# The broadcast of C in a state-space scan: full precision matmuls from one copy of its rows, and C first in every step

## The reference, cut to what matters

```
x (4,256,256), ctx (4,256,128);  DI = 256 channels, DS = 16 states, L = 256 times
u      = silu(causal_conv4(in_proj @ ctx))                  per batch: 256 channels x 256 times
B, C   = x_proj @ u                                         16 rows each, x 256 times
delta  = softplus(dt_proj @ (x_proj_dt @ u) + bias)
state[t] = state[t-1] * exp(delta[t] * A) + delta[t] * u[t] * B[t]     for every channel and state n
y[t]   = sum over n of state[t] * C[t]  + D * u[t]
x1     = x + y * silu(layernorm(x))
logits = layernorm(x1) @ Wg;  the best 2 of 8 experts by softmax, at most 320 rows for each
out    = x1 + sum over the 2 of weight * (relu(row @ w1) @ w2)
```

## Time and profile before

| | |
|---|---|
| median of 3 runs | 289.02 us (288.33 to 290.1) |
| the profiled execution, its own time | 288.53 us |
| its span, first to last instruction | 286.7 us |
| busy: PE, DVE, ACT, POOL | 84%, 75%, 61%, 74% of the span |
| mean granted clock of TensorE | 0.93 of full speed |

### The profile page before, as it was taken

One profiled execution on the slowest core, in us unless ns is written; L12 is line 12 of the kernel. 1 busy time (PEld: TensorE's weight loads), 2 busy tenths in 40 slices (PEclk: granted clock), 3 DMA queues, 4 the chain that ended last, 5 costly groups with the idle time before them and its releaser, 6 DMA issues.

```text
span 286.7 us, 5022 instructions
## 1 busy us (share of the span) xinstructions
PE 239.6 (84%) x1564; PEld 218.4 (76%) x1564; DVE 216.1 (75%) x372; ACT 174.1 (61%) x379; POOL 213.5 (74%) x174
## 2 busy tenths in 40 slices
PE   8967597867957396678699999999999999999970
PEld 7745476545845285557589999999999999999960
DVE  3799999999799999999978757566675738383620
ACT  2899759777886776669326357463747465564400
POOL 1689899669976999998744668687777777777561
PEclk9999959995999957589999999999999999999995
DMA  6679520080002805043032675745544454544110
GB/s 158 236 224 330 215 120 0 5 305 25 0 1 67 303 0 187 0 145 112 21 129 74 205 235 186 231 169 205 174 178 169 178 173 179 213 181 182 38 59 24
DMA packets 15073, 40.38 MB, mean 141 GB/s; under 512 B 2922, under 2 KB 9900, under 8 KB 12112
## 3 DMA queue, kind: packets, MB, share of 16 engines
q1 hardware_dynamic: 11792, 33.15, 33.9%
q0 software_dynamic: 2816, 6.32, 6.6%
q10 hardware_dynamic: 448, 0.70, 0.9%
HBM read 32.72 MB, written 8.49 MB: 144 GB/s over the span
## 4 chain that ended last, share of the span: by engine, by line
PE 39%; issue 4%; DVE 4%; DMA 2%; POOL 2%; ACT 1%; POOLq 1%; SPq 0%; ACTq 0%
PE ps L1064 12%; PE ps L1065 11%; PE ps L1066 11%; DVE h L1291 2%; PE ps L1073 2%; PE ps L1080 2%; DVE hc L1303 1%; DMA xe<-expert_rows 1%; DMA expert_rows<-xrow,sloti 1%; POOL expert_rows L403 1%; POOL so_far L482 1%; POOL out L491 1%; DMA out<-eo,dst 1%; POOLq L108 1%; DVE eo L1497 0%
## 5 line engine op out<-in xcount | busy, mean ns | idle before, releaser
L358 POOL TENSOR_TENSOR dbu<-du,bsb 128x1024 f32<-128x1024 f32 x31 | 72.7, 2366 | 1.2 <-DMA bsb<-b_rows 1.0
L582 ACT ACTIVATE ps<-delta,anegs 128x255 f32<-128x255 f32 x128 | 53.0, 461 | 14.4 <-DVE h L1284 10.7
L1486 DVE SCALAR_TENSOR_TENSOR htlo<-ps,hthi 128x320 fp32r<-128x320 f32 x64 | 30.4, 487 | 37.8 <-ACT hthi L748 37.8
L847 PE MATMUL ps<-stack,sels 64*128 64x256 f32 x64 | 17.2, 355 | 34.9 <-DVE hc L1303 32.1
L847 PEld LDWEIGHTS ps<-stack,sels 64*128 64x128 f32 x64 | 11.0, 215 | 42.7 <-issue 42.3
L472 POOL TENSOR_TENSOR w2lo<-w2raw,w2hi 128x512 fp32r<-128x512 f32 x28 | 35.9, 1302 | 9.0 <-ACT w2hi L643 8.8
L869 PE MATMUL ps<-cst,hc 128*128 128x128 f32 x256 | 40.7, 310 | 1.4 <-DVE hc L1303 1.4
L1284 DVE TENSOR_TENSOR_SCAN h<-ps,dbu 128x1024 f32<-128x1024 f32 x18 | 41.1, 2283 | 0.4 <-POOL dbu L358 0.3
L1064 PE MATMUL ps<-xthi,w1hi 128*128 (+1 forms) x124 | 39.3, 317 | 0.3 <-ACT w1hi L636 0.3
L748 ACT ACTIVATE hthi<-ps 128x320 fp32r<-128x320 f32 x64 | 28.0, 437 | 18.6 <-PE ps L1066 18.6
L1303 DVE TENSOR_TENSOR hc<-h,ps 128x1024 f32<-128x1024 f32 x31 | 37.1, 1197 | 2.6 <-issue 2.0
(11 more groups left out here) (185 smaller groups left out, 510.4 us busy)
## 6 DMA issues: line engine op xcount, KB each, us to landing
w1raw<-in_w SPq DMA_DIRECT2D x8, 1024.0 KB
w2raw<-in_w SPq DMA_DIRECT2D x8, 1024.0 KB, 4.9
bsb<-b_rows SPq DMA_DIRECT2D x7, 1024.0 KB, 6.6
expert_rows<-fill SPq DMA_DIRECT2D x1, 2580.0 KB, 15.8
xe<-expert_rows SPq DMA_DIRECT2D x8, 258.0 KB, 5.1
out<-x SPq DMA_DIRECT2D x4, 256.0 KB, 5.1
xnat<-in_x SPq DMA_DIRECT2D x1, 768.0 KB, 7.3
xe<-expert_rows SPq DMA_DIRECT2D x8, 64.5 KB, 5.2
```

The source lines that it names most:

```text
L358: nc.gpsimd.tensor_tensor(dbu[j % DRING][:], du[:, :, None, cols(b)].to_broadcast([P, EC, 2, L]), bsb[b % 2][:, None, 2 * p:2 * p + 2, :]. ...
L582: ins = nc.scalar.activation(decays(g % SLOTS_DA)[:, c, i * L + 1:(i + 1) * L], delta[:, c, b * L + 1:(b + 1) * L], ACT.Exp, scale=anegs[: ...
L1486: nc.vector.scalar_tensor_tensor(out=htlo[:, f, :], in0=ps[:, f % 4, 0:CAP], scalar=0.0, in1=hthi[:, f, :].bitcast(F32), op0=ALU.max, op1= ...
```

## The change

The rows of B and C are copied once, in full precision, by one ScalarE instruction (`copy_rows`); `hi_rows`, `lo_rows` and the doubled projection go. C is spread by full precision matmuls from 32 rows. On TensorE c_cast(g+1) now stands first in the step, ahead of `logits` and `counts`, and the convolution is cut into three pieces (p = 3, 4, 5). The bank of its own goes to the last step but one, whose mult comes ahead of the last scan. The sum of the exponentials comes from ScalarE's accumulator, and GpSimd takes the inverse (a power of -1) and multiplies (`weigh`). Where other lines of the diff only follow from these, they are left out.

```diff
 def c_bank(g):
-    return WBANK if g == STEPS - 1 else CBANK
+    return WBANK if g == STEPS - 2 else CBANK
...
-        sels = sm("sels", [XPC, BC], F32R)
-        stack = sm("stack", [XPC, T], F32R)
-        brow = sm("brow", [XPC, L])
+        sels = sm("sels", [BC, BC])
+        rows = sm("rows", [BC, T])
...
+            def weigh(b):
+                pool.wait_ge(s["top_exp"], b + 1)
+                pool.wait_ge(s["const_done"], 1)
+                tiles = tiles_of(b)
+                nc.gpsimd.tensor_tensor(rsum[:, tiles], rsum[:, tiles], none1[:, tiles], ALU.pow
+                                        ).then_inc(s["sum_inverse"], 1)
+                pool.wait_ge(s["sum_inverse"], b + 1)
+                nc.gpsimd.tensor_tensor(xrow[:, tiles, :, DM], etop[:, tiles, 0:TOPK],
+                                        rsum[:, tiles, None].to_broadcast([P, BT, TOPK]), ALU.mult
+                                        ).then_inc(s["gates_done"], 1)
...
                 if b == 2 and p in (1, 5):
                     if p == 1:
                         pool.wait_ge(s["xe_filled"], 16)
+                        weigh(0)
                     send(0 if p == 1 else 1)
+                if b == 3 and p == 2:
+                    weigh(1)
                 if b == 3 and p in (2, 3):
                     send(p)
                 drive(j)
...
+            weigh(B - 2)
             for j in tiles_range(B - 2):
                 send(j)
...
-            def hi_rows(b):
-                nc.scalar.activation(stack[:, cols(b)], ps[0:XPC, XBANK[b], 0:L], ACT.Copy).then_inc(s["hi_done"], 1)
-
-            def b_rows(b):
+            def copy_rows(b):
                 act.wait_ge(s["xp_psum"], b + 1)
-                if b:
-                    act.wait_ge(s["brow_out"], 16 * b)
-                nc.scalar.activation(brow[0:DS, :], ps[0:DS, XBANK[b], 0:L], ACT.Copy).then_inc(s["brow_done"], 1)
+                nc.scalar.activation(rows[:, cols(b)], ps[0:BC, XBANK[b], 0:L], ACT.Copy).then_inc(s["rows_done"], 1)
...
                     ins = nc.scalar.activation(etop[:, j, :], top[:, j, :], ACT.Exp, bias=ntop[:, j:j + 1],
-                                               scale=rx[:, j:j + 1])
+                                               scale=rx[:, j:j + 1], accum_out=rsum[:, j:j + 1])
...
             def c_cast(g):
                 b, p = divmod(g, PAIRS)
-                pe.wait_ge(s["stack_done"], b + 1)
-                if g == STEPS - 1:
+                pe.wait_ge(s["rows_done"], b + 1)
+                if g == STEPS - 2:
                     pe.wait_ge(s["zt_done"], B)
+                elif g == STEPS - 1:
+                    pe.wait_ge(s["mult_done"], g - 1)
                 elif g:
                     pe.wait_ge(s["mult_done"], g)
...
-                                           stack[:, cols(b)], start=(i == 0), stop=True, skip_group_check=True)
+                                           rows[:, cols(b)], start=(i == 0), stop=True, skip_group_check=True)
...
             for g in range(STEPS):
                 b, p = divmod(g, PAIRS)
                 nb = b + 1
+                if g + 1 < STEPS - 1:
+                    c_cast(g + 1)
+                if g == STEPS - 3:
+                    c_cast(STEPS - 1)
                 if b >= 1:
                     if p == (3 if b == B - 1 else 4):
                         logits(b - 1)
                     if p == (4 if b == B - 1 else 6):
                         counts(b - 1)
-                if g + 1 < STEPS - 1:
-                    c_cast(g + 1)
-                if g == STEPS - 3:
-                    c_cast(STEPS - 1)
...
-                if b + 2 < B and p in (3, 4):
+                if b + 2 < B and p == 3:
                     pe.wait_ge(s["sp_t"], nb + 1)
-                    conv(b + 2, p - 3, WBANK)
+                    conv(b + 2, 0, WBANK, range(0, 3))
+                if b + 2 < B and p == 4:
+                    conv(b + 2, 0, WBANK, range(3, TAPS))
+                    conv(b + 2, 1, WBANK, range(0, 2))
+                if b + 2 < B and p == 5:
+                    conv(b + 2, 1, WBANK, range(2, TAPS))
...
             scan(0)
-            lo_rows(0)
             for g in range(STEPS):
                 b, p = divmod(g, PAIRS)
-                if g + 1 < STEPS:
+                if g < STEPS - 2:
                     scan(g + 1)
-                mult(g)
+                    mult(g)
+                else:
+                    mult(g)
+                    if g + 1 < STEPS:
+                        scan(g + 1)
                 nb = b + 1
-                if nb < B:
-                    if p == (1 if b else 2):
-                        lo_rows(nb)
...
-                    if p == (5 if b == B - 1 else 7):
-                        sum_weights(b - 1)
```

More of the change, by code:

```diff
@@ L57 @@
 BC = 2 * DS
-XPC = 2 * BC
 WP = 4
@@ L129, in build @@
         nhalf = sb("nhalf", [P, TILES])
+        none1 = sb("none1", [P, TILES])
         stats = sb("stats", [P, TILES, 6])
@@ L174, in build @@
         ctxs = sm("ctxs", [DC, T])
-        xps = sm("xps", [P, EC, XPC])
+        xps = sm("xps", [P, EC, BC])
         u = sm("u", [P, EC, T])
@@ L244, in spread_b @@
             def spread_b(b):
-                sp.wait_ge(s["brow_done"], b + 1)
-                sp.dma_start(b_dram[b], brow[0:DS, :]).then_inc(s["brow_out"], 16)
+                sp.wait_ge(s["rows_done"], b + 1)
+                sp.dma_start(b_dram[b], rows[0:DS, cols(b)]).then_inc(s["brow_out"], 16)
                 sp.wait_ge(s["brow_out"], 16 * (b + 1))
@@ L319, in _ @@
             nc.gpsimd.memset(nhalf[:], -0.5)
+            nc.gpsimd.memset(none1[:], -1.0)
             nc.gpsimd.memset(fill[:, 0:DM + 1], 0.0)
@@ L450, in _ @@
             pool.wait_ge(s["xe_in"], 32)
[L451 to L454, removed]
+            weigh(B - 1)
             pool.wait_ge(s["gates_done"], B)
@@ L785, in x_proj @@
             def x_proj(b, c, bank):
-                return nc.tensor.matmul(ps[0:XPC, bank, 0:L], xps[:, c, :], u[:, c, cols(b)],
+                return nc.tensor.matmul(ps[0:BC, bank, 0:L], xps[:, c, :], u[:, c, cols(b)],
                                         start=(c == 0), stop=(c == EC - 1))
@@ L808, in first_dt, with conv @@
                 return ins
-            def conv(b, c, bank):
+            def conv(b, c, bank, taps=range(TAPS)):
                 acc = by_chunk(bank)[:, c, :]
-                for k in range(TAPS):
+                for k in taps:
                     ins = nc.tensor.matmul(acc[:, k:L], cwb[:, TAPS - 1 - k, c * P:(c + 1) * P],
@@ L815, in conv @@
                                            stop=(k == TAPS - 1), skip_group_check=True)
-                if c == EC - 1:
+                if c == EC - 1 and taps[-1] == TAPS - 1:
                     ins.then_inc(s["conv_psum"], 1)
@@ L846, in c_cast @@
                     n = DS + 2 * p + i
-                    ins = nc.tensor.matmul(ps[:, c_bank(g), i * L:(i + 1) * L], sels[:, n:n + 1].to_broadcast([XPC, P]),
-                                           stack[:, cols(b)], start=(i == 0), stop=True, skip_group_check=True)
+                    ins = nc.tensor.matmul(ps[:, c_bank(g), i * L:(i + 1) * L], sels[:, n:n + 1].to_broadcast([BC, P]),
+                                           rows[:, cols(b)], start=(i == 0), stop=True, skip_group_check=True)
                 ins.then_inc(s["c_psum"], 1)
@@ L961, in _ @@
             conv(1, 0, YBANK)
[L962 to L963 removed]
+            pe.wait_ge(s["sel_in"], 16)
             c_cast(0)
@@ L991, in _ @@
                 add_state(g).then_inc(s["ysum_done"], 1)
-                if b == B - 1 and p in (2, 3, 4, 5):
+                if b == B - 1 and p in (2, 3, 4, 5, 6):
                     if p == 2:
                         pe.wait_ge(s["fill_made"], 1)
-                    add_zeros((4, 4, 6, 2)[p - 2])
+                    add_zeros((4, 4, 6, 2, 6)[p - 2])
                 if b == 0 and p == 1:
@@ L1211, in z_variance @@
                 ins.then_inc(s["z_stats"], 1)
-            def lo_rows(b):
-                dve.wait_ge(s["hi_done"], b + 1)
-                dve.wait_ge(s["brow_done"], b + 1)
-                nc.vector.tensor_tensor(stack[BC:2 * BC, cols(b)], ps[BC:2 * BC, XBANK[b], 0:L],
-                                        stack[BC:2 * BC, cols(b)].bitcast(F32), ALU.subtract
-                                        ).then_inc(s["stack_done"], 1)
             def softplus_t(b, bank):
@@ L1388, in place @@
                 nc.vector.tensor_copy(sloti[:, tiles, :], slot).then_inc(s["slots_done"], 1)
-            def sum_weights(b):
-                tiles = tiles_of(b)
-                dve.wait_ge(s["top_exp"], b + 1)
-                link(nc.vector.tensor_reduce(rsum[:, tiles], etop[:, tiles, :], AX.X, ALU.add))
-                nc.vector.reciprocal(rsum[:, tiles], rsum[:, tiles]).then_inc(s["weights_sum"], 1)
             def low_w1(e, m):
@@ L1453, in _ @@
             place(last)
-            sum_weights(last)
```

33 lines of the change are left out of this document (9 added, 24 removed).

## The result

The changed kernel takes 310.81 us (median of 4 runs; 288.97 for the kernel before beside them), a ratio of 1.0751 with an interval of 1.0707 to 1.0795. Forecast was 295.3, with a range of 291 to 299: the direction was right, but the rise of 6.3 that was forecast is less than a third of the one that came. The profiled span is 308.4, 21.7 more than the 286.7 of before.

What follows compares the result with a forecast made beforehand. VectorE was taken to bound the scan stage. At 2.4 GHz, -2.45 - 2.6 + 7.7 + 0.95 + 0.5 = +4.1; with 1.2 GHz stretches +9.25; the middle, +6.7, gave 295.3 us, range 291 to 299.

Steps and rivals of the forecast that it cites:

- the clock: TensorE in the scan stage: more C instructions mean less idling, favouring 2.4 GHz; middle of +4.1 and +9.25 taken, +6.7.
- The upper end, +9.25: Sum of all terms if TensorE runs at 1.2 GHz in the same stretches as before.
- The prediction's own sign of being wrong: One of three listed: VectorE's waits for C at 1.2 GHz outweigh its waits for the counts.
- What goes off VectorE: Scan stage: `lo_rows` gone saves 0.45 in batches 1 to 3, `sum_weights` 0.30 three times, start 0 to 0.45; -2.45.
- The two late C: Mults 5 and 13 waited 0.59 and 2.00 for C behind a slow convolution; -2.6 at 2.4 GHz, bound +0.35.
- The price of a C: A pair on TensorE goes from 0.47 to 0.94 in four instructions, free in the plain step, at 1.2 GHz just so.
- The rival of a cheap pair: C's four instructions on 32 rows take 0.47 together, so the kernel is not slower: 290.2; chance 0.07.
- The new waits: VectorE waits at `place` and `choose` because logits and counts stand behind C: four waits, +7.7, the largest term.
- ScalarE's turn: Batch 2's convolution ends some 1.6 later, 0.67 of it slack, delaying the scan of step 9: +0.95.
- GpSimd: `weigh` delays drives behind its first call: +0.5; new VectorE waits cover the rest, without that cover up to 1.5 more.
- a clock that stays up: Rival: TensorE stays at 2.4 GHz throughout, so only +4.1, 292.6; chance 0.22.
- The late C stay late: Rival: low-clock stretches stay where they are, C stays late and the new waits grow, 297.8; chance 0.15.

Runs made afterwards that it cites:

- e6: Changed kernel with logits and counts ahead of C again, C padded to 128 rows, convolution in two chunks and weights on ScalarE as before: 289.37 us.
- e7: As e6, but without the padding, so C in full precision on 32 rows: 303.05 us.
- e9: As e6 with its 128-row copy, projection and loads, but C's matmuls read only the first 32 rows: 300.76 us.
- e1: Changed kernel with C's copy and selector padded from 32 to 128 rows with zeros, no instruction added or moved: 297.49 us.
- e14: As e1, plus products with zeros on 128 rows filling TensorE's waits: 295.56 us.
- e12: As e6, but C of the next step ahead of logits and counts, as in the change: +8.4 us against the kernel before.
- e5: Changed kernel with C on 128 rows and logits and counts ahead of C again: +4.7 us against the kernel before.
- e11: As e6, but the weights made on GpSimd (power and product) as in the change: 294.09 us.
- e13: As e6, but C's copy and selector on 96 rows instead of 128: 291.14 us.

## Why the prediction was wrong

**The step that failed is the clock**, "I take the middle, +6.7", and the reason ahead of it: "TensorE has four instructions for C in each of the 32 steps in place of two, so it idles less, which speaks for 2.4 GHz". Busy time was taken for what keeps the clock up. C in full precision is busy for twice as long but on 32 rows, and e6, e7 and e9 show that such time does not hold the clock: low time went from 34 to 61 us and not down. The upper end, +9.25, assumed the low stretches of before as the worst case; it was no bound. In the +6.7 the clock had a share of 2.6 (6.7 less the 4.1 at 2.4 GHz). Measured, C's rows alone are worth 13.1 (the change less e1) or 13.8 (e7 less e6) of the 21.7, and rows and filled waits together 15.1 (the change less e14). The prediction's own sign of being wrong came true: VectorE waits 9.6 for C and 7.8 for the counts.

**What goes off VectorE**: right, if anything too small. In e14, against before, the mult behind each place of `lo_rows` comes 0.71, 0.57 and 0.57 nearer (forecast 0.45 each), and behind two places of `sum_weights` 0.31 and 0.32 (forecast 0.30). Not all of it reaches the end: in e6 the last mult starts 1.5 earlier than before and the first expert's rows are turned 1.0 earlier, but the span is 0.3 longer. The 0.2 at the start cannot be read: mult 0 starts 0.47 earlier in the change and 0.95 later in e14.

**The two late C**: right at 2.4 GHz. In e14 mult 5 gains 0.67 on before and mult 13 2.08 (forecast 0.59 and 2.00). At 1.2 GHz, in the change, mults wait 9.6, because the low stretches lie at other steps and are longer.

**The price of a C**: 0.94 was forecast; 1.05 pass from C's start to that of the sums in the change at full clock:

```profile
44.30 1.12 PE L841 MATMUL ps<-rows,sels 32*128 32x256 f32 x4
45.35 1.09 PE L863 MATMUL ps<-cst,hc 128*128 128x128 f32 x8
```

The rival of a cheap pair is excluded. That it "fits" at 1.2 GHz is a second error: C alone does, but C and sums at 2.07 and 1.97 are longer than the step and leave no room for logits, z or counts.

**The new waits**: right, in place and in size once the clock is up. The first `place` waits 1.79 in e14, forecast 1.79; all of `place` and `choose` 8.5, forecast 7.7. In the change they are 11.5, and 8.6 (e12 less e6) is what the order costs alone, e12's longer low time (31 us against 14) included.

**ScalarE's turn**: seen in place, of unsteady size. The scan of step 9 waits 0.43 in the change, 0.62 in e14 and 1.33 in e5, where 0.95 was forecast; e6 and e11, with conv as before, have no such wait, but e7 has 0.42.

**GpSimd**: power and product take 0.71 and 0.21, as taken. The wait of +0.5 behind them is not confirmed: scans wait for drives there for 0 in the change, 0.42 in e14, 0.52 in e11 and 2.17 in e5, and for 0.46 in e6, which has no `weigh` on GpSimd. Without the cover e11 is 6.1 above e6, four times the 1.5 given as bound; of its profiled 4.2, 1.0 is the later arrival of the first expert's rows, and 3.2 is lost at mults that are as late in e13, without that `weigh`.

**The rivals**: a clock that stays up was given +4.1; e14, with 14 us of low clock left, is at +6.6 (5.2 to 8.1), so the other terms together were some 1.1 to 4.0 too small at most. "The late C stay late" named part of what happened, C late at a low clock, but took the low stretches as before and a price that was too low. The rule on transposes that the prediction took from the Trainium skill ("TensorE: Matmul & The Clock Gate", Part 4) had been used for 2.4 GHz; the clock fell, and no run here separates transposes.

**The sums**: three small slips, none of which changes the outcome. The terms given for mult 13 at 1.2 GHz make it 0.4 to 0.5 earlier and not 0.25. The wait for drives goes up to 0.96 (1.9 less 0.94) and not 0.75. With the median 0.49 above the profiled execution, 295.2 becomes 295.7 and not 295.3.

## What to carry to other kernels

When a change makes TensorE's instructions longer on few rows, don't count the added busy time as a gain for the clock: ask how much work on all rows is left in each stretch, and cost the step at both clocks, with no assumption that the low stretches stay where they were. Padding a matmul's contraction with rows of zeros cost C no time on TensorE (1.10 on 128 rows, 1.12 on 32) and was worth 13 us here. When one part of a change is priced by taking it back alone, look at where the low stretches lie in both profiles before the difference is put down to that part: e11 is 6.1 above e6, but no more than 1.0 of it is seen to come from GpSimd's weights.

## What the hardware showed that was not expected

With C in four instructions of full precision, reading 32 or 64 rows did not hold the clock (+12.5 to +13.6, 48 to 55 us low), reading 96 or 128 did (+0.9 and -0.2, 24 and 14 us low), with the same count of instructions. TensorE can stay at 1.2 GHz for 34 us while it is busy for 30.16 of 34.20. The exact point between 64 and 96 rows, whether the kind of full-row work matters, and why two rounded instructions on 64 rows do no harm (34 us low in the kernel before) stay open.
